# Six expert groups requested earlier, in landing places of their own, in an adapter-plus-expert feed-forward kernel

## The reference, cut to what matters

```
B_sel = B[adapter_ids];  A_sel = A[adapter_ids]             # 8 batches, 8 adapters of rank 16
c     = (x @ B_sel^T) @ A_sel^T                             # x: 8 x 512 x 2048, f32
base_out   = c @ base_w^T + base_b                          # 2048 x 2048
res_hidden = c @ A^T                                        # rank 64
probs      = softmax(c @ router_w^T)                        # 16 experts
topw, topi = top_k(probs, 2);  topw = topw / (sum(topw) + 1e-6)
combine    = sum(one_hot(topi) * topw)
delta      = einsum('bse,bsr,eor->bso', combine, res_hidden, B_experts)   # 16 x 2048 x 64
out        = x + base_out + delta * 0.5
```

## Time and profile before

| | |
|---|---|
| median of 3 runs | 467.74 us (467.37 to 468.12) |
| the profiled execution | 468.7 us, of which the span from first to last instruction is 466.3 us |
| PE busy | 414.2 us, 89% of the span |
| DVE busy | 312.8 us, 67% |
| ACT busy | 107.6 us, 23% |
| mean granted PE clock | 0.985 of full speed |
| transfers | 135.30 MB, mean 290 GB/s |

### The profile page before, as it was taken

One profiled execution on the slowest core, in us unless ns is written; L12 is line 12 of the kernel. 1 busy time (PEld: TensorE's weight loads), 2 busy tenths in 40 slices (PEclk: granted clock), 3 DMA queues, 4 the chain that ended last, 5 costly groups with the idle time before them and its releaser, 6 DMA issues.

```text
span 466.3 us, 6141 instructions
## 1 busy us (share of the span) xinstructions
PE 414.2 (89%) x2240; PEld 275.4 (59%) x2240; DVE 312.8 (67%) x702; ACT 107.6 (23%) x163; POOL 48.1 (10%) x54
## 2 busy tenths in 40 slices
PE   0577997699749999999999999999999999999996
PEld 0456885476535575566556656755665566566675
DVE  2699799788534566756776676777557766757353
ACT  0002034254524331023012202310230132122210
POOL 3720000011000012012001200110120012002000
PEclk9998999899988999999999999999999999999999
DMA  8999999799979698799889889998897899655844
GB/s 235 363 337 335 335 376 362 245 249 280 326 222 269 206 353 319 259 293 360 269 294 341 315 272 300 363 334 278 287 357 271 287 339 323 227 193 189 290 174 181
DMA packets 90292, 135.30 MB, mean 290 GB/s; under 512 B 5461, under 2 KB 43349, under 8 KB 90261
## 3 DMA queue, kind: packets, MB, share of 16 engines
q1 hardware_dynamic: 63588, 102.07, 65.2%
q10 hardware_dynamic: 26674, 32.84, 23.0%
HBM read 99.24 MB, written 35.65 MB: 289 GB/s over the span
## 4 chain that ended last, share of the span: by engine, by line
PE 66%; DVE 16%; DMA 11%; issue 2%; ACTq 2%; SPq 1%; ACT 1%; DVEq 0%
PE ps L870 13%; PE ps L889 12%; PE ps L890 10%; PE ps L891 10%; DMA early_u<-in_L_ffn_B 7%; PE ps L902 7%; DVE early L639 5%; PE ps L892 5%; DMA xbuf<-in_L_ffn_base_w 5%; DVE xT L705 3%; PE ps L835 3%; DVE h_r L686 3%; PE ps L825 3%; DVE xbuf L813 2%; PE ps L913 1%
## 5 line engine op out<-in xcount | busy, mean ns | idle before, releaser
L813 DVE TENSOR_TENSOR xbuf<-ps,xbuf 128x512 f32<-128x512 f32 x128 | 87.0, 680 | 118.2 <-PE ps L892 118.1
L889 PE MATMUL ps<-h_r,u_r 128*128 128x512 f32 x256 | 109.6, 428 | 7.0 <-DVE xbuf L813 7.0
L890 PE MATMUL ps<-h_r,u_r 128*128 128x512 f32 x256 | 100.4, 392 | 0.0
L891 PE MATMUL ps<-h_r,u_r 128*128 128x512 f32 x256 | 100.1, 391 | 0.0
L835 PE MATMUL ps<-early 128*128 128x256 f32 x256 | 63.7, 400 | 22.1 <-DVE early L639 22.1
L889 PEld LDWEIGHTS ps<-h_r,u_r 128*128 128x128 f32 x256 | 48.0, 188 | 47.6 <-issue 20.1
L705 DVE STREAM_TRANSPOSE xT<-xbuf 128x512 f32<-128x512 f32 x112 | 72.1, 682 | 0.0
L639 DVE STREAM_TRANSPOSE early<-xbuf 128x256 f32<-128x256 f32 x128 | 66.0, 598 | 7.3 <-issue 4.0
L835 PEld LDWEIGHTS ps<-early 128*128 128x128 f32 x256 | 48.2, 199 | 34.1 <-issue 16.8
L870 PE MATMUL ps<-bexpT,cur 128*32 128x512 f32 x512 | 63.2, 612 | 2.2 <-DVE h_r L686 1.5
L471 ACT ACTIVATE h_r<-ps 128x512 fp32r<-128x512 f32 x64 | 35.8, 594 | 87.4 <-issue 54.7
(11 more groups left out here) (65 smaller groups left out, 210.7 us busy)
## 6 DMA issues: line engine op xcount, KB each, us to landing
out<-xbuf SPq DMA_DIRECT2D x31, 1024.0 KB, 7.0
xbuf<-in_x SPq DMA_DIRECT2D x28, 1024.0 KB, 6.9
xbuf<-in_x SPq DMA_DIRECT2D x32, 512.0 KB, 8.4
xbuf<-in_x ACTq DMA_DIRECT2D x32, 512.0 KB, 9.5
xbuf<-in_L_ffn_base_w SPq DMA_DIRECT2D x16, 512.0 KB, 18.4
xbuf<-in_L_ffn_base_w ACTq DMA_DIRECT2D x16, 512.0 KB, 19.0
gm_r<-g_hilo SPq DMA_DIRECT2D x128, 32.0 KB, 6.1
early_u<-in_L_ffn_B SPq DMA_DIRECT2D x15, 256.0 KB, 12.5
```

The source lines that it names most:

```text
L813: dve.tensor_tensor(xs, ps[:, ACC + t % 2, :], xs, ALU.add).then_inc(s_out, 1)
L889: pe.matmul(acc, u_r[:, b.q, 0, h, tok_t], hi, start=(h == 0), stop=False)
L890: pe.matmul(acc, u_r[:, b.q, 0, h, tok_t], lo, start=False, stop=False)
L891: pe.matmul(acc, u_r[:, b.q, 1, h, tok_t], hi, start=False, stop=False)
```

## The change

It has four parts.

1. `E_SLOT` gives groups 10 to 13 places of their own: slots 3 and 4 in the upper half of `xT` (free when the first batch's x products are done, `s_bxq`), slots 5 and 6 in the last block of `bexpT`, where batch 0's x lay (free when that is flipped, `s_xe`). Groups 14 and 15 use slots 0 and 1, whose last users are groups 9 and 7.
2. The requests move. ACT no longer requests a half inside `copy_experts`, ahead of the two copies, but at the W-stage positions of `E_LOAD_AT`. SP's order is written anew, and in both queues all sixteen groups are requested before the W stage ends.
3. The bias comes as 16 rows of 128 in one transfer, POOL converts it on 16 partitions, and two small transfers put the high and the low part into rows 64 and 96 of `gm_r`.
4. Each store of G has a semaphore of its own, so that a block of `gm_r` waits only for its own quarter. `e_where` also swaps the order of the two inner indices, so that the groups that land in `bexpT` are flipped before their place is written.

```diff
-        e_in = e_early + [xT[:, XRING // 2:XRING // 2 + 2, :].rearrange("p a t -> p (a t)")
-                          .rearrange("p (a m) -> p a m", a=EG)]
+        e_in = (e_early + [xT[:, a:a + 2, :].rearrange("p a t -> p (a t)").rearrange("p (a m) -> p a m", a=EG)
+                           for a in (XRING // 2, XRING // 2 + 2)]
+                + [bexpT[:, OC - 1, a:a + 2, :].rearrange("p a o -> p (a o)").rearrange("p (a m) -> p a m", a=EG)
+                   for a in (NP // 2, NP // 2 + 2)])
...
-        bias_n = xT[:, XRING // 2:, :].rearrange("p a t -> p (a t)")
+        BR = O // P
+        bias_n = xT[0:BR, XRING // 2, 0:3 * P].rearrange("p (a t) -> p a t", t=P)
...
-        E_SLOT = (0, 1, 2, 0, 1, 2, 0, 1, 2, 0, 1, 3, 0, 1, 0, 1)
-        E_FRESH, EIN_AT = 11, 104
-        PIECE_AT, X0_AT = {26: 5, 51: 6, 63: 7}, 31
+        E_SLOT = (0, 1, 2, 0, 1, 2, 0, 1, 2, 0, 3, 4, 5, 6, 0, 1)
+        E_LOAD_AT = {31: 3, 50: 4, 62: 5, 75: 6, 83: 7, 89: 8, 93: 9, 102: 10, 103: 11, 106: 12, 110: 13, 117: 14, 120: 15}
+        PIECE_AT, X0_AT = {26: 5, 51: 6, 63: 7}, 32
-        XRES_AT, XQ_AT = {96: 0, 109: 1, 118: 2}, 113
+        XRES_AT, XQ_AT = {97: 0, 112: 1, 119: 2}, 108
...
-            return g // PER_C, g // 2 % 2, g % 2
+            return g // PER_C, g % 2, g // 2 % 2
...
             if e_users(g):
                 eng.wait_ge(s_ef, e_users(g)[-1] + 1)
-            elif g == E_FRESH:
+            elif g in (10, 11):
                 eng.wait_ge(s_bxq, KD)
+            elif g in (12, 13):
+                eng.wait_ge(s_xe, KD)
...
             def load_gm(b, c):
 
+                if b == 0:
+                    sp.wait_ge(s_gst[c], 16)
...
-            for row in (64, 96):
-                sp.dma_start(bias_n[row:row + 1, :], base_b.rearrange("(a o) -> a o", a=1)).then_inc(s_bias, 16)
+            sp.dma_start(bias_n[:, 0, :], base_b.rearrange("(a o) -> a o", a=BR)).then_inc(s_bias, 16)
...
             load_experts(sp, 1, 0)
+            sp.wait_ge(s_biaslo, 1)
+            sp.wait_ge(s_const, 2)
+            for part, row in ((1, 64), (2, 96)):
+                sp.dma_start(f32(gm_r[row:row + 1, :]).rearrange("a (p t) -> a p t", t=P), bias_n[:, part, :])\
+                  .then_inc(s_biasrow, 16)
...
             load_first_xres(sp, 0, 0)
+            load_gm(0, 0)
             load_experts(sp, 10, 0)
-            sp.wait_ge(s_gst, 32)
-            for c in range(2):
-                load_gm(0, c)
+            load_experts(sp, 11, 0)
             store_g(2)
-            load_experts(sp, 11, 0)
-            load_first_xres(sp, 1, 0)
+            load_experts(sp, 12, 0)
             sp.wait_ge(s_wt, 7 * KD)
             load_xquad(sp, 1, 0, (0, 1))
-            load_experts(sp, 12, 0)
+            load_experts(sp, 13, 0)
+            load_first_xres(sp, 1, 0)
+            load_gm(0, 1)
+            load_experts(sp, 14, 0)
             load_first_xres(sp, 2, 0)
-            sp.wait_ge(s_gst, 48)
-            load_gm(0, 2)
+            load_experts(sp, 15, 0)
             sp.wait_ge(s_wt, 8 * KD)
             load_xquad(sp, 1, 1, (0, 1))
             store_g(3)
-            load_experts(sp, 13, 0)
             load_first_xres(sp, 3, 0)
-            load_experts(sp, 14, 0)
-            sp.wait_ge(s_gst, 64)
+            load_gm(0, 2)
             load_gm(0, 3)
-            load_experts(sp, 15, 0)
...
-            for n, row in enumerate((64, 96)):
-                pool.tensor_copy(gm_r[row:row + 1, :], bias_n[row:row + 1, :]).then_inc(s_biashi, 1)
-                pool.wait_ge(s_biashi, n + 1)
-            pool.tensor_tensor(gm_r[96:97, :], bias_n[96:97, :], f32(gm_r[96:97, :]), ALU.subtract)\
+            pool.tensor_copy(bias_n[:, 1, :].bitcast(F32R), bias_n[:, 0, :]).then_inc(s_biashi, 1)
+            pool.wait_ge(s_biashi, 1)
+            pool.tensor_tensor(bias_n[:, 2, :].bitcast(F32R), bias_n[:, 0, :], bias_n[:, 1, :], ALU.subtract)\
...
                 act.wait_ge(s_ef, g + 1)
-                for k in e_next(g):
-                    load_experts(act, k, 1)
...
             for n in range(NW):
+                if n in E_LOAD_AT:
+                    load_experts(act, E_LOAD_AT[n], 1)
...
-                if n == EIN_AT:
-                    load_experts(act, E_FRESH, 1)
...
-                if f.n == 1 and j == XRING // 2:
-                    dve.wait_ge(s_ef, max(g for g in range(GROUPS) if E_SLOT[g] == E_SLOT[E_FRESH]) + 1)
+                if f.n == 1 and j in (4, 6):
+                    dve.wait_ge(s_ef, E_SLOT.index(j // 2 + 1) + 1)
```

More of the change, by code:

```diff
@@ L160, in adaln_ffn @@
         s_load = [[sem(f"w_loaded{k}_half{h}") for k in range(WB)] for h in range(2)]
-        s_ein = [sem(f"expert_in{k}") for k in range(4)]
+        s_ein = [sem(f"expert_in{k}") for k in range(7)]
         s_ef, s_ec = sem("experts_flipped"), sem("experts_copied")
@@ L166, in adaln_ffn @@
         s_xquad = [sem(f"xquad{g}") for g in range(2)]
-        s_gst, s_gm = sem("g_stored"), [sem(f"gm{c}") for c in range(NC)]
-        s_biashi, s_biaslo = sem("bias_hi"), sem("bias_lo")
+        s_gst, s_gm = [sem(f"g_stored{g}") for g in range(W_GROUPS)], [sem(f"gm{c}") for c in range(NC)]
+        s_biashi, s_biaslo, s_biasrow = sem("bias_hi"), sem("bias_lo"), sem("bias_rows")
         s_a = sem("a_copied")
@@ L214, in adaln_ffn @@
         E_LATE = {0: 10, 1: 11, 2: 12, 3: 13, 5: 14, 6: 15}
-        E_SLOT = (0, 1, 2, 0, 1, 2, 0, 1, 2, 0, 1, 3, 0, 1, 0, 1)
-        E_FRESH, EIN_AT = 11, 104
-        PIECE_AT, X0_AT = {26: 5, 51: 6, 63: 7}, 31
+        E_SLOT = (0, 1, 2, 0, 1, 2, 0, 1, 2, 0, 3, 4, 5, 6, 0, 1)
+        E_LOAD_AT = {31: 3, 50: 4, 62: 5, 75: 6, 83: 7, 89: 8, 93: 9, 102: 10, 103: 11, 106: 12, 110: 13, 117: 14, 120: 15}
+        PIECE_AT, X0_AT = {26: 5, 51: 6, 63: 7}, 32
         GLO_AT = 40
-        XRES_AT, XQ_AT = {96: 0, 109: 1, 118: 2}, 113
+        XRES_AT, XQ_AT = {97: 0, 112: 1, 119: 2}, 108
         EB = 0
         def e_where(g):
-            return g // PER_C, g // 2 % 2, g % 2
+            return g // PER_C, g % 2, g // 2 % 2
         def e_users(g):
             return [k for k in range(g) if E_SLOT[k] == E_SLOT[g]]
-        def e_next(g):
-            return [k for k in range(g + 1, GROUPS) if E_SLOT[k] == E_SLOT[g]][:1]
         def load_experts(eng, g, h):
@@ L312, in store_g @@
                 sp.dma_start(g_dram[:, :, g * BANK:(g + 1) * BANK].rearrange("l p o -> p l o"),
-                             g_out[g]).then_inc(s_gst, 16)
+                             g_out[g]).then_inc(s_gst[g], 16)
             def load_gm(b, c):
+                if b == 0:
+                    sp.wait_ge(s_gst[c], 16)
                 for rep in range(2):
@@ L424, in _ @@
             ids = [adapter(pool, b) for b in range(NB)]
-            pool.wait_ge(s_a, NB)
-            pool.wait_ge(s_bias, 32)
-            for n, row in enumerate((64, 96)):
-                pool.tensor_copy(gm_r[row:row + 1, :], bias_n[row:row + 1, :]).then_inc(s_biashi, 1)
-                pool.wait_ge(s_biashi, n + 1)
-            pool.tensor_tensor(gm_r[96:97, :], bias_n[96:97, :], f32(gm_r[96:97, :]), ALU.subtract)\
+            pool.wait_ge(s_bias, 16)
+            pool.tensor_copy(bias_n[:, 1, :].bitcast(F32R), bias_n[:, 0, :]).then_inc(s_biashi, 1)
+            pool.wait_ge(s_biashi, 1)
+            pool.tensor_tensor(bias_n[:, 2, :].bitcast(F32R), bias_n[:, 0, :], bias_n[:, 1, :], ALU.subtract)\
                 .then_inc(s_biaslo, 1)
@@ L526, in slot @@
                     if f.n < 2:
-                        act.wait_ge(s_gst, 16 * W_GROUPS if f.n == 1 else 32)
+                        act.wait_ge(s_gst[2 * f.n + 1], 16)
                     need(act, s_ulo, f.n * 2)
@@ L571, in _ @@
                     if SLOT_AT[n] in UP_AT:
-                        act.wait_ge(s_gst, 16 * (W_GROUPS - 1))
+                        act.wait_ge(s_gst[2], 16)
                     slot(first, SLOT_AT[n], False)
@@ L672, in take_g @@
                 dve.wait_ge(s_wmm, (g + 1) * 2 * KD)
-                need(dve, s_gst, 16 * (g - 1))
+                if g >= 2:
+                    dve.wait_ge(s_gst[g - 2], 16)
                 dve.tensor_copy(g_out[g][:, 0, :].bitcast(F32R), ps[:, ACC + g % 2, :]).then_inc(s_ghi, 1)
@@ L788, in _ @@
                     if j == XRING // 2:
-                        dve.wait_ge(s_biaslo, 1)
+                        dve.wait_ge(s_biasrow, 32)
                     x_transpose(first, j)
@@ L876, in tile_products @@
                 acc = ps[:, ACC + t % 2, :]
+                if b.n == 0 and m == 0:
+                    pe.wait_ge(s_biasrow, 32)
                 if m == 0:
```

## The result

The changed kernel took 460.88 us (median of 6 runs, 459.41 to 463.04), against 467.93 us (467.37 to 470.34) for the kernel before in the same comparison: a ratio of 0.9845 with a 95% interval of 0.9808 to 0.9882. It is faster by 1.2 to 1.9%, and the time lies in the forecast's range of 457.3 to 462.8 us, 1.5 us above its 459.4. Its profiled execution took 459.67 us with a span of 457.4, against a forecast of 458.0 for the span.

The account below looks back on a forecast made before the run. PE was taken to bound the kernel, stalled in batch 0 by group 13's late transfer. Wait 5.9 plus slow clock 2.6 less cost 0.2 made 8.3 us: median 467.7 to 459.4 us, range 457.3 to 462.8.

Parts of the forecast that it names:

- What bounds it: PE, busy 414.2 of 466.3 us; gains only in its gaps, chiefly group 13's late transfer of 15.03 us.
- The wait, 5.9 us: Batch 0: group 13, requested early, lands in time; its flips start at 131.59 in place of 137.48, saving 5.89 us.
- The step by step shift: ACT's copy of group 10 begins 0.66 us earlier without the request; group 11's flips move from 125.34 to 124.68.
- The slow clock, 2.6 us: Behind group 13's wait: at full clock flips, h and bx products take 4.53 us, not 7.15; bounds 0 to 2.6.
- (a): W stage, n = 102 and 103: two requests ahead of the copy into `tmp` lose 0.2 us, bounds 0 and 1.9.
- (b): Bias: two more tiny transfers early in SP's queue and shorter POOL work cost nothing, 0.3 us either way.
- (c): Requests of groups 6 to 9 follow ACT's copies instead of leading them: nothing, or up to 1 us.
- a sign of being wrong: PE's wait at 87.7 us, ahead of batch 0, having changed length would show the forecast wrong.
- The other signs: Batch 0 flips not ended by transfers, clock 1.00 from 92 to 180 us, tile 4 8 to 9 us earlier.
- The queue behind: Second pair of x quarters, behind 1.57 MB more, lands at 136.9, wanted at 138.6: cover 1.7 us, nothing lost.
- the sum: Whole kernel: 5.9 + 2.6 - 0.2 = 8.3 us saved, median from 467.7 to 459.4 us.
- The first rival: Late x quarters, the `tmp` copy's 1.9 us or the clock give part back: 460.4 to 464 us, chance 0.23.

Follow-up runs that it names:

- the filler: Kernel before, with 48 transposes of the identity into a free bank ahead of group 13's flips, so PE works through the wait: 465.01 us, ratio 0.9958.
- the second measurement: The changed kernel measured once more, unaltered, beside the kernel with milder later flips of groups 5 to 9: 460.47 us, ratio 0.9877.

## Why the prediction was right

**What bounds it.** Right, and sharpened: the stall at group 13 was the gain, and no more. One request put back takes all of it by the time (ratio 1.0016) and 6.0 of 8.5 us by the length, two others put back take 0.7 us in the profile, the bias and the semaphores bring nothing.

**The wait, 5.9 us.** Forecast from 137.48 to 131.59, measured to 131.28, of which 0.23 us is the earlier start of the stage. The step by step shift was right too: without the request the copy of group 10 starts 0.02 us after the flips, and group 11's idle time went from 1.41 to 0.73 us.

**The slow clock, 2.6 us.** 7.15 us became 4.63 in the changed kernel (131.28 to 135.91), 2.5 less, and the filler alone, with the late transfer, gave 4.46. The Trainium skill, in TensorE: Matmul & The Clock Gate, What's actually happening, says that activity releases the throttle. The traces agree: in 137.5 to 141 us the clock was 1.00 behind transposes of the identity, and 0.50 behind idle time.

**The costs.** (a) 0.2 us for the copy into `tmp`: measured 0.3. (The upper bound of 1.9 should have been 1.8, 101.3 less 99.54.) (b) and (c) were put at nothing, and the h copy, 0.23 us earlier than before, seems to confirm it. That is luck in part. Group 6's flips start 1.12 us later than before (88.86 and not 87.74), and from there to the h copy it is 1.35 us less, because flips and W products behind them ran at full clock this time (1.09 + 3.02 us and not 1.72 + 4.08), less the 0.3 of (a). The wait at 87.7 has changed length, which I had named as a sign of being wrong: 1.72 + 4.15 us for groups 5 and 6 became 3.56 + 2.41. The other profiles show such shifts without any change there, so I don't read it as an effect of the change. But (b), forecast at nothing with 0.3 us either way, measured a loss of 0.4 to 2.9 us when run alone, and no profile shows where. The other signs came as forecast: no flip of batch 0 waits for a transfer, the clock is 1.00 in 92 to 180 us, tile 4 starts 8.7 us earlier, and the weights from `tmp` are loaded at 99.43.

**The queue behind.** This is the step that was wrong in its place, though it did not change the sum. I named the second pair of x quarters as the thinnest cover, landing at 136.9 and wanted at 138.6. They landed at 134.7 (117.5 + 17.2) and were wanted at 138.4: the bytes moved ahead cost 2.5 us, not 4.7, and 3.7 us were left. The thin cover was at ACT, 0.3 us in this profile and none in others, in the time that ACT spends on issuing. I priced a request at 0.6 to 1.5 us, as in the earlier trace rows, and did not ask what it costs when more is queued. The first rival had a slow request in its list, but at `tmp` and not here. The Trainium skill, in DMA: Bandwidth & Descriptors, Issuing engines are not separate DMA queues, says that the requests of both engines interleave on the same 16 DMA engines. The traces agree: with 1 and 3 extra transfers in SP's queue, ACT's request took 6.01 and 11.20 us in place of 3.72.

**The median.** 460.9 us measured, 459.4 forecast; the profiled executions of the changed kernel gave 459.7 and 460.0. So the forecast's 8.3 us fits the profiled pair, which lost 8.9 us of span, better than the medians, which lost 7.1 (by the ratios it is 7.3, and 5.7 in the second measurement). The range held, the size was somewhat too large. What is missing is not in the stage that the sum was made of: its length fell by 8.5 us in both profiles. It may lie in the spread between runs, which the profile of before gave no reason to expect, or in the loss that the bias and the semaphores showed alone. That it lies ahead of batch 0 is likely, since nothing behind tile 4 moved in any profile, but only one or two runs of each kernel were profiled, and no experiment explained it.

## What to carry to other kernels

Look for the request that waits for a consumer just ahead of its own use, and give that transfer a free place: of six groups moved, putting one back took the whole gain away. Where a stall leaves PE idle, add the work done slowly behind it to its price, here 2.6 us on 5.9. And before queueing more transfers, look at what stands behind a request on the engine that issues it: that engine's own work, not the landing, may have the thinnest cover.

## What the runs showed of the hardware

A request is not a fixed cost. One request of the same 512 KB on ACT took 1.46 us before and 0.60 in the filler run, whose code is that of before up to there, 3.72 and 3.28 in two profiles of the changed kernel, 0.60 with groups 14 and 15 taken out of the queue ahead of it, 6.01 with 1 MB more in the other queue and 11.20 with 3 MB more, and ACT executed nothing that stands behind it meanwhile: in the last two cases it idled 6.37 and 11.57 us. SP shows the same: its store of G's last quarter took 0.38 us to issue before, 3.82 after and 11.91 with 3 MB more. That store landed 11.7 us after its request before and 17.7 after.
